# A graph and mixture-of-experts kernel: one small expert block moved ahead of the loop, two loads moved ahead of a scatter chain, five sums moved from GpSimd to accumulating transfers

## What is computed

```python
e = jnp.einsum('ehd,hd->eh', act, att)
m = jax.ops.segment_max(e, dst, num_segments=n)
p = jnp.exp(e - m[dst])
...
out = jax.ops.segment_sum(alpha[..., None] * xl[src], dst, num_segments=n)
```

```python
def _lresnet(x, y, w):
    z = x + w * y
    inner = -z[..., :1] ** 2 + jnp.sum(z[..., 1:] ** 2, -1, keepdims=True)
    return jnp.sqrt(C) * z / jnp.sqrt(jnp.clip(-inner, EPS))
...
y, _ = jax.lax.scan(step, y0, (We1, be1, We3, be3, We2, be2, w_te.T, hit_te.T))
z = _lmlp(xt, Ws1, bs1, Ws3, bs3, Ws2, bs2)
out = _lresnet(y, z, 1.0)
```

## Time and profile before

| | us |
|---|---|
| median of the runs shown (1774.0 to 1775.93) | 1774.23 |
| the profiled execution | 1774.9 |
| its span | 1773.0 |
| TensorE busy (97% of the span) | 1719.4 |
| VectorE busy | 745.7 |
| GpSimd busy | 646.0 |
| ScalarE busy | 396.3 |

### The profile page before, as it was taken

The page is one execution under the profiler, slowest core; times in us unless marked ns, Lnnn a source line. Parts: engine busy times, 40 slices in busy tenths (PEclk is TensorE's granted clock), DMA queues, the critical chain, the costliest instruction groups (busy, mean ns, idle before and its releaser), DMA issues. The chain is left out here.

```text
span 1773.0 us, 20965 instructions
## 1 busy us (share of the span) xinstructions
PE 1719.4 (97%) x8008; PEld 1071.3 (60%) x8008; DVE 745.7 (42%) x1548; ACT 396.3 (22%) x740; POOL 646.0 (36%) x535
## 2 busy tenths in 40 slices
PE   9999999998999999999999999999999999999996
PEld 6466445544444677755477775556777667766642
DVE  5886011422732432155455554853332322222238
ACT  1000000001411000110177772832100222222132
POOL 0666883031000046767788862000210322222203
PEclk9999999998999999999899999999999999999998
DMA  9654116074170034333322222814353999999941
GB/s 345 203 164 126 2 3 165 1 212 119 68 300 5 0 99 120 100 96 100 88 53 59 53 45 64 209 48 157 88 169 127 378 400 416 411 410 400 370 122 58
DMA packets 103673, 281.44 MB, mean 159 GB/s; under 512 B 61728, under 2 KB 69138, under 8 KB 91201
## 3 DMA queue, kind: packets, MB, share of 16 engines
q1 hardware_dynamic: 28755, 218.54, 33.6%
q0 software_dynamic: 67792, 50.53, 13.0%
q10 hardware_dynamic: 7050, 11.34, 2.0%
HBM read 250.10 MB, written 29.80 MB: 158 GB/s over the span
## 5 line engine op out<-in xcount | busy, mean ns | idle before, releaser
L608 POOL DMA_INDIRECT table_d<-wring x85 | 173.4, 2040 | 105.6 <-issue 67.4
L380 PE MATMUL bank<-wring,region_a 128*125 128x512 f32 x480 | 207.6, 593 | 1.6 <-DVE region_a L754 0.7
L993 POOL DMA_INDIRECT wring<-xl_d,wring x85 | 109.5, 1289 | 257.3 <-DMA xr_d<-flat_b 231.4
L380 PEld LDWEIGHTS bank<-wring,region_a 128*125 128x125 f32 x480 | 89.7, 188 | 115.2 <-issue 114.2
L2393 PEld LDWEIGHTS bank<-picked_t,wring 128*128 128x128 f32 x1152 | 131.0, 194 | 10.8 <-issue 10.8
L1006 POOL DMA_INDIRECT score_d<-wring x85 | 110.2, 1297 | 73.7 <-DMA score_d<-wring 45.7
L2393 PE MATMUL bank<-picked_t,wring 128*128 128x128 f32 x1152 | 132.9, 278 | 3.7 <-issue 3.7
L396 PE MATMUL bank<-flat_d,wring 128*128 128x312 f32 (+1 forms) x512 | 135.0, 426 | 0.0
L396 PEld LDWEIGHTS bank<-flat_d,wring 128*128 128x128 f32 x512 | 97.0, 189 | 37.7
L993 POOL DMA_INDIRECT wring<-xr_d,wring x85 | 107.9, 1270 | 25.9 <-issue 24.1
L2400 PE MATMUL bank<-wring,small_t 128*64 128x256 f32 x640 | 73.3, 382 | 2.7 <-issue 2.7
(11 more groups left out here) (441 smaller groups left out, 2675.8 us busy)
## 6 DMA issues: line engine op xcount, KB each, us to landing
wring<-in_experts SPq DMA_DIRECT2D x57, 2048.0 KB, 13.3
wring<-in_L_Ws SPq DMA_DIRECT2D x6, 2048.0 KB, 11.2
table_d<-eq_buf SPq DMA_DIRECT2D x2, 3072.0 KB, 28.3
score_d<-no_edge SPq DMA_DIRECT2D x2, 3072.0 KB, 32.0
wring<-table_d POOLq DMA_DIRECT2D x10, 610.4 KB, 7.4
wring<-score_d SPq DMA_DIRECT2D x5, 1093.8 KB
wring<-pid_d ACTq DMA_DIRECT2D x17, 312.5 KB, 4.0
wring<-in_edge_w ACTq DMA_DIRECT2D x17, 312.5 KB, 4.5
```

Source lines behind the costliest of these rows:

```text
L380: ins = pe.matmul(bank[0:R, :], act_t[:, k, tok(t)], w[:, k * HALF:(k + 1) * HALF], start=(k == 0), stop=(k == chunks - 1))
L608: pool.indirect_dma_start(out=tables_d[b % 2], out_offset=bass.IndirectOffsetOnAxis(ap=edge_at[:, b:b + 1], axis=0), in_=edge_sums[:, b, : ...
L993: pool.indirect_dma_start(out=to[:, g % 2, j, :], out_offset=None, in_=table, in_offset=bass.IndirectOffsetOnAxis(ap=index[:, b:b + 1], ax ...
```

## The change

1. **Edge stage.** The counts of tiles 0 and 1 and the bias `bo` are loaded as soon as the last group of logits is made, and no longer between and behind the first scores.
2. **Expert stage.** The extra small block becomes block 0 of the small ones and runs ahead of the loop (`first_block`), around the gate product of big block 0. Turn i then has big block i and small block i + 1. Its gate and up weights go into slots 4 and 5, its down weights into slot 2; slots 4, 2 and 5 are loaded for turn 0 when it has used them. Behind the loop only the shared expert's ten halves are left on TensorE. VectorE takes the picks' dots ahead of the first shared halves, and the last three bank uses of the shared halves are in another order; picks and shared rows change places in SBUF.
3. **Tail.** GpSimd's five adds become five transfers from SBUF to SBUF that add to their destination (`accum_op`), issued by GpSimd. The sum now lands in `mixed`, which VectorE's dot reads, so a transfer waits for that dot (`rows_dotted`), which is announced for rows 0 to 2 together. GpSimd waits for each transfer before it issues the next.

The diff, cut to its core:

```diff
+                sp.wait_ge(logits_made, GROUPS_E + 1)
+                for t in range(2):
+                    load_counts(t)
+                sp.wait_ge(hsem["q_used"], UNITS)
+                sp.dma_start(bo, a["L1_bo"].to_broadcast([R, D]).rearrange("r (a c) -> r a c", a=2)).then_inc(bias_in, 16)
                 sp.wait_ge(scores_out, 16 * EB)
                 for t in range(2):
                     load_scores(t)
-                    load_counts(t)
-                sp.wait_ge(hsem["q_used"], UNITS)
-                sp.dma_start(bo, a["L1_bo"].to_broadcast([R, D]).rearrange("r (a c) -> r a c", a=2)).then_inc(bias_in, 16)
...
-                small_expert = sp.value_load(expert_i[0:1, 1, 0:1], min_val=0, max_val=NE1 - 1)
+                first_small = sp.value_load(expert_i[0:1, 1, 0:1], min_val=0, max_val=NE1 - 1)
+                small_expert = sp.value_load(expert_i[0:1, 1, 1:2], min_val=0, max_val=NE1 - 1)
+                load_expert(sp, first_small, 0, 4)
+                load_expert(sp, first_small, 1, 5)
                 sp.wait_ge(*wt.freed[-4])
                 load_expert(sp, expert, 0, 0)
-                load_expert(sp, small_expert, 1, 4)
-                load_expert(sp, small_expert, 2, 5)
                 sp.wait_ge(*wt.freed[-3])
                 load_expert(sp, expert, 1, 1)
                 sp.wait_ge(*wt.freed[-2])
-                load_expert(sp, expert, 2, 2)
+                load_expert(sp, first_small, 2, 2)
...
+                def first_block():
+                    pe.wait_ge(small_picked, 1)
+                    small_product(weights(4, -1), 0)
+                    small_product(weights(5, -1), 1).then_inc(gu_filled, 1)
+                    big_gate(0)
+                    pe.wait_ge(small_made, 1)
+                    turn_units()
+                    pe.wait_ge(small_squared, 1)
+                    sum_units()
+                    pe.wait_ge(small_in, 32)
+                    turn_small(pe, bank_ts)
+                    for (at, n), bank in zip(TOKEN_PIECES, (bank_o0, bank_o1)):
+                        pe.matmul(bank[0:1, 0:n], ones[:, 0:1], sq_sum[:, at:at + n], start=True, stop=True)\
+                            .then_inc(s_filled, 1)
+                    small_down(weights(2, -1), 0)
...
+                    if not first:
+                        big_gate(i)
...
-                small_product(weights(3, turns), 0)
-                small_product(weights(4, turns), 1).then_inc(gu_filled, 1)
-                pe.wait_ge(time_made, 2)
-                halves = [weights(0, turns)]
-                shared_half(0, range(4))
-                pe.wait_ge(small_made, turns + 1)
-                turn_units()
-                pe.wait_ge(small_squared, turns + 1)
-                sum_units()
-                shared_half(0, range(4, K)).then_inc(d_filled, 1)
-                pe.wait_ge(os_made, turns)
-                pe.wait_ge(small_turned, turns + 1)
-                pe.wait_ge(small_timed, turns + 1)
-                small_down(weights(5, turns)).then_inc(os_filled, 1)
-                halves.append(weights(1, turns))
...
+                small_hidden(0)
+                small_time(0)
+                v.wait_ge(ts_filled, 2)
+                keep_small(v, bank_ts)
+                for n, ((at, cols), bank) in enumerate(zip(TOKEN_PIECES, (bank_o0, bank_o1))):
+                    v.wait_ge(s_filled, TIME_FROM + n + 1)
+                    v.tensor_scalar(hid_t[0:1, 0, at:at + cols], bank[0:1, 0:cols], 1.0, 1e-6, ALU.add, ALU.max)\
+                        .then_inc(time_clipped, 1)
+                small_rows_out(0)
...
-                    v.wait_ge(z_made, added)
-                    tiny(summed[:, t, 0:1], small[:, Y0, t:t + 1], small[:, T3, t:t + 1], ALU.add)
+                    v.wait_ge(z_made, 16 * added)
+                    tiny(mixed[:, t, 0:1], small[:, Y0, t:t + 1], small[:, T3, t:t + 1], ALU.add)
...
-                small_hidden(turns)
-                small_time(turns)
+                dot_picks(0)
                 take_shared(0)
-                v.wait_ge(small_stored, turns * 16)
-                small_rows_out(turns)
+                dot_picks(1)
                 take_shared(1)
-                dot_picks(0)
+                dot_picks(2)
+                dot_picks(3)
                 take_shared(2)
-                dot_picks(1)
-                dot_picks(2)
-                take_shared(3)
-                dot_picks(3)
...
+                v.sem_inc(rows_dotted, 3)
...
+                pool.wait_ge(ts_filled, 1)
+                gather(pool, small_rows, node_of[0:SMALL, 1, 1, 0:1], small_in)
+                pool.wait_ge(rows_in_all, 16)
+                pool.partition_broadcast(small_bias[:], bias_row[:, D:]).then_inc(biases_spread, 1)
                 pool.wait_ge(ta_filled, 1)
                 pool.wait_ge(tb_filled, 1)
                 gather(pool, picked, node_of[:, 0, 1, 0:1], picked_in)
-                pool.wait_ge(ts_filled, 1)
-                gather(pool, small_rows, node_of[0:SMALL, 1, 1, 0:1], small_in)
+                pool.wait_ge(places_made, 4)
+                pool.tensor_copy(place_of[:, 1:2], small_place[:, 0:1]).then_inc(index_copied, 1)
+                pool.wait_ge(index_copied, 1)
+                pool.wait_ge(ts_filled, 2)
+                gather(pool, small_rows, node_of[0:SMALL, 1, 2, 0:1], small_in)
+                pool.wait_ge(os_made, 1)
+                scatter_small()
...
-                pool.wait_ge(small_stored, turns * 16)
-                pool.tensor_copy(place_of[:, 1:2], small_place[:, bass.ds(turns, 1)]).then_inc(index_copied, 1)
-                pool.wait_ge(index_copied, turns * 4 + 1)
-                pool.wait_ge(os_made, turns + 1)
-                pool.sem_inc(rows_ready, 1)
-                pool.indirect_dma_start(out=routed_halves,
-                                        out_offset=bass.IndirectOffsetOnAxis(ap=place_of[:, 1:2], axis=0),
-                                        in_=small_out[:], in_offset=None).then_inc(small_stored, 16)
...
-                    pool.tensor_tensor(summed[:, t, cols], mixed[:, t, cols], shared_out[:, t, cols], ALU.add)\
-                        .then_inc(z_made, 1)
+                    pool.wait_ge(rows_dotted, t + 1)
+                    pool.dma_start(mixed[:, t, cols], shared_out[:, t, cols], accum_op=ALU.add).then_inc(z_made, 16)
+                    pool.wait_ge(z_made, 16 * t + 16)
...
+                expert = sp.value_load(expert_i[0:1, 0, 0:1], min_val=0, max_val=NE1 - 1)
+                small_expert = sp.value_load(expert_i[0:1, 1, 1:2], min_val=0, max_val=NE1 - 1)
+                sp.wait_ge(gu_filled, 1)
+                load_expert(sp, small_expert, 1, 4)
+                sp.wait_ge(os_filled, 1)
+                load_expert(sp, expert, 2, 2)
+                load_expert(sp, small_expert, 2, 5)
...
-                sp.wait_ge(gu_filled, turns)
-                load_expert(sp, small_expert, 0, 3)
-                load_expert(sp, small_expert, 1, 4)
-                sp.wait_ge(os_filled, turns)
-                load_expert(sp, small_expert, 2, 5)
```

More of the change, by code:

```diff
@@ L2027, in gps_kernel @@
         expert_rows = a["experts"].rearrange("(m p) c -> m p c", p=P)
-        SLOT_LOADS = [wt.loads(slot, len(wt.sources)) for slot in range(SLOTS_W)]
+        SLOT_LOADS = [wt.loads(slot, len(wt.sources)) + (slot in (2, 4, 5)) for slot in range(SLOTS_W)]
         def load_expert(sp, expert, m, slot):
@@ L2435, in routed @@
                     ins.then_inc(g_filled, 1)
-                    if first:
-                        for (at, n), bank in zip(TOKEN_PIECES, (bank_o0, bank_o1)):
-                            pe.matmul(bank[0:1, 0:n], ones[:, 0:1], sq_sum[:, at:at + n], start=True, stop=True)\
-                                .then_inc(s_filled, 1)
-                    pe.wait_ge(small_picked, i + 1)
+                def first_block():
[13 more added lines that the diff above has]
+                    small_down(weights(2, -1), 0)
+                def routed(i, first):
+                    if not first:
+                        big_gate(i)
+                    pe.wait_ge(small_picked, i + 2)
                     for n, ins in big_product(weights(1, i), up_part):
@@ L2444, in routed @@
                     pe.wait_ge(picked_in, 16 * i + 32)
-                    if not first:
-                        pe.wait_ge(os_made, i)
+                    pe.wait_ge(os_made, i + 1)
                     turn_big(pe)
@@ L2474, in _ @@
+                first_block()
                 turns = turn_loop(pe, routed)
-                def shared_half(n, ks):
+                pe.wait_ge(time_made, 2)
+                halves = [None, None]
+                for n in range(2 * T):
                     t, h = n // 2, n % 2
-                    for k in ks:
+                    if n < 2:
+                        halves[h] = weights(h, turns)
+                    if n == 1:
+                        pe.wait_ge(small_picked, turns + 2)
```

(26 more changed lines are left out.)

154 lines of the change are left out of this document (75 added, 79 removed).

## The result

The changed kernel takes **1787.09 us** (median of 5 runs, 1784.6 to 1791.7) against 1774.0 us of the kernel before beside it: ratio 1.0079, 95% interval 1.006 to 1.0097. It is slower by 13 us; the prediction was 1775.3 us with a range up to 1782. The profiled execution took 1787.09 us, its span is 1785.3 us, 12.3 more than before.

What follows compares the result with a forecast made beforehand. TensorE, busy 97% of 1773.0 us, was taken as the bound, with VectorE last in the tail. Terms +3.3 (edge), 0 (loop), -2.5 (tail) and 0.3 (new waits) gave +1.1: 1775.3 us on the median, range 1767.5 to 1782.

Steps and rivals of the forecast that it cites:

- Edge stage, +3.3 (0 to 5.3): Edge stage: 1.75 MB of early loads delay GpSimd's chain of score scatters, and TensorE with it, by 3.3 us.
- TensorE's first softmax wait from 3.7 to 7: Edge stage, a sign: TensorE's wait at the first softmax grows from 3.7 to 7 us; if it stays, that step is wrong.
- Small block first, loop end +12.0, nothing else: Expert loop: the block's work ahead of it ends the loop 12.0 us later; late loads cost 0, from 0 to +5.
- the starved first block: Expert loop, rival: slots 2, 5 and 0 arrive late, costing 3 to 6 us once, 1779 to 1781; chance 0.06.
- Tail up to T0, 8.7 earlier: Tail: T0, the closing of rows 0 to 2, comes at 1733.3 instead of 1742.0, with TensorE's shared half 5 late.
- Sums by accumulating transfers, T0 + 33.5: Tail: at 4.5 us per transfer the end comes 33.5 us after rows 0 to 2 close, before 27.3; tail -2.5.
- the upper bound of 11.5: Tail: highest price allowed for one accumulating transfer, 11.5 us, the earliest landing of accumulating loads from HBM.
- the slow case: Tail: accumulating transfers at 6 us each instead of 4.5, giving +7 in all, 1781.3 us.
- slower: the sums are the bound: Tail, rival: 6 us per transfer, end at T0 + 39.5, 1781.3 us; chance 0.24 for slow transfers or scatters.
- the slow scatters: Edge stage, rival: scatters held up by 5.3 us give 1777.3 us; chance 0.24 for slow transfers or scatters.

Runs made afterwards that it cites:

- e10_counts_only: Kernel before the change, with only the edge counts and output bias loaded early, ahead of the last scatters: 1779.64 us, ratio 1.0029.
- e6_plain_copy: Changed kernel with plain copies of the same shape in place of the accumulating transfers, sums left out: 1772.45 us, ratio 0.9987.
- e8_stores_last: Changed kernel with result rows 0 to 2 stored only when row 3 is finished: 1787.19 us, ratio 1.0067.

## Why the prediction was wrong, point by point

*Edge stage, +3.3 (0 to 5.3): right mechanism, size not settled.* The last scatter starts at 1097 and not at 1093.7, as forecast, 0.7 us of it by luck, since this trace was late by so much beforehand. In the profiled run the stage cost 2.2 us. Over the eight traces it is 4.4 in the mean, over medians 2.1 to 5.8: the value taken may be a microsecond or two short, the upper bound nearly right. The forecast had added one single hold-up; in half of the traces two scatters in a row are held up.

*TensorE's first softmax wait from 3.7 to 7: wrong for the profiled run.* Its two waits sum to 4.62 us, 4.05 before; in `e10_counts_only` to 8.25. By the forecast's own sign the step would be refuted, but TensorE does become later by what VectorE does (2.2 us): the other 1.6 us of the cost are its 16 products at the lower granted clock (0.52 and 3.59 us, instead of 1.00 and 2.01). The prediction hadn't reckoned with the clock.

*Small block first, loop end +12.0, nothing else: right, 1.2 us too much.* It is 10.7 to 10.9 in all kernels that have it. TensorE never waits for the loads, so the starved first block is out; the loads' longer way (19.8 us instead of some 14) stayed inside the slack.

*Tail up to T0, 8.7 earlier: right within a microsecond.* It came at 1736.66; less the 2.9 us by which this trace was late at the start of the expert stage, that is 1733.8, 8.2 earlier, forecast 1733.3. The dots are at 1.22 us, and the half that the closing waits for is TensorE's, as said. With the adds kept the block is worth 9 us, 8 by stages.

*Sums by accumulating transfers, T0 + 33.5: **the step that failed**.* T0 + 45.3 was measured (1781.9 - 1736.66). The term is the price of one transfer, 4.5 us, with 1 more beside stores. Sums 0, 1 and 2 were forecast at T0 + 4.6, 9.2 and 14.8; they were used at 7.4, 16.1 and 24.5. Row 3's was forecast at 23.9 and came at 35.5; the last at 30.9 and 42.9. So 9.7 of the 11.8 us were lost on the first three, 1.9 on the fourth and 0.4 on the fifth, and 0.2 came back behind it. These 11.8 us are the whole miss of the forecast, 1787.1 against 1775.3. Inside the term:

- The bytes. I had taken 2.5 us for 512 KB, from 207 GB/s of five accumulating loads from HBM that were queued together. A lone transfer between two places of SBUF moves at 98 GB/s, some 5.2 us. `e6_plain_copy` shows that 4.5 us is about a plain copy's price (4.2 us, 14.2 at sum 2), and that 2.5 us more is the accumulation's, on each row. That the total fits the copy is in part luck: its bytes took 3.4 us and not 2.5, and what was added to them, 2.1 us, was too much.
- The row behind the 207. The window of the earlier trace rows holds two queues: of its 1.75 MB the accumulating loads moved 1.45, which is 181 GB/s at a share of 0.92, so 197 and not 207. The 2.2 us taken off for the plain copy stand in no row; its packets' share in the trace gives 2.4. Both slips are small and cancel. Idle engines explain 0.9 us of the lone row's 5.2 (share 0.82). The rest is that busy engines moved less, 120 GB/s against 197; three queued rows reach 154. So a full queue explains a part of the difference, and the rest is not shown. As a value 2.5 us was unfounded, it was a bound; the upper bound of 11.5 was in the text, but my range gave the slow case only 6 us.
- The stores. 1 us was allowed; they cost 2.0 and 1.6 on two transfers (8.5 and 8.1 against 6.5 in `e8_stores_last`).
- The path. The five transfers exceed their forecast prices (4.5, 4.5, 5.5, 5.5, 4.1) by 2.3, 4.0, 2.6, 1.5 and -0.1 us, 10.3 in all, and nothing hides it, since each stands on the path; the other 1.5 us are small steps between, such as the 0.55 us from the closing step to the first issue.

The Trainium skill ("DMA: Bandwidth & Descriptors", Anatomy of one DMA — SWDGE (gpsimd) path) gives, as an estimate by its fit, 3.2 us for such a transfer. The runs show 4.2 for the plain copy and 6.7 for the accumulating one, so here the measurement decides against it.

*The rival "slower: the sums are the bound"* was the true case: 1781.3 at 6 us each, decisive from about 5. With T0 + 45.3 in place of its T0 + 39.5 its sum gives 1787.1, the measured time. It had a chance of 0.24 together with the slow scatters, and its price, too, was taken from plain copies (5.5 to 7.2 us).

## What to carry to other kernels

Moving work from an engine to a transfer pays only if the transfer's whole way from issue to landing is off the path. Here four dependent transfers of 7 to 8.5 us and one of 4 took the place of adds of 3.3 and 1.7 us that nobody waited for. A rate read from other transfers, queued and with another source, was no rate for a lone one. A chain of small transfers (scatters that wait for each other) was held up by 1.75 MB of loads put ahead of it, hardly by 0.6 MB, and how much shows only over many executions. A wait of TensorE can cost more than its length, when the products behind it run at the lower clock. Of a change of three parts each is worth a run by itself: here one part alone, the small block first, is 9 us faster than the kernel before.

## What the runs showed of the hardware

- Accumulating from SBUF into SBUF, 125 rows of 4 KB over GpSimd's queue: 6.5 to 6.8 us from issue to use alone, 8.1 to 8.5 beside stores of results; for rows of 2 KB 4.0 alone and 7.6 beside stores. A plain copy of the same shape: 4.2 and 2.8 us from issue to landing.
- The accumulation moved 98 to 106 GB/s alone, 137 with three rows queued, 105 with pieces of half the size. With the engines busy throughout this would be 120, 154 and 133. The accumulating loads from HBM in the kernel before moved 181 GB/s beside another queue (1.45 MB in the 8 us of the earlier trace rows, 197 with all engines); how much of the difference is the source and how much the longer queue was not tried.
- 1.75 MB of loads issued 0.3 us behind a scatter's issue held up that scatter and the next (waits of 4.4 to 4.5 and 5.0 to 5.1 us instead of some 1.6 and 2.2); issued 1.8 to 2.5 us behind, only one (6.6 to 7.6). Why is open. With 0.6 MB issued 2.5 us behind, the wait was 3.15.
- TensorE's granted clock after an idle time: behind a wait of 2.50 us the next 16 products ran at 0.52 (1.2 GHz) and took 3.59 us; behind 0.34 us, before the change, at 1.00 (2.4 GHz) and 2.01 us.
